# Attention and FFN layer on one core: V projected into token rows for two head pairs, output projection and next x's transposes as fillers, PV visits and fillers replanned

## What is computed

```python
q, k, v = x @ w_q, x @ w_k, x @ w_v                  # per head, 128 -> 64
probs   = softmax(q @ k.T / 8 + causal_mask)         # 1024 x 1024 per head
attn    = sum over heads of (probs @ v) @ w_o.T
x1      = layernorm(x + attn)
h       = butterfly(x1 @ W_exp + b_exp, up_weights)   # 9 stages over 512 features
y       = butterfly(gelu(h + up_bias), down_weights) @ W_con + b_con + down_bias
out     = layernorm(x1 + y)
```

## Time and profile before

| | |
|---|---|
| median of three runs | 1208.28 us |
| profiled execution | 1209.85 us, span of its instructions 1207.8 us |
| PE matmul busy | 1124.5 us, 93% of the span |
| PE weight loads busy | 725.1 us, 60% |
| DVE, ACT, POOL busy | 728.8, 650.3, 758.4 us (60%, 54%, 63%) |
| mean granted PE clock | 0.982 of full speed |
| chain that ended last | PE 69%, DMA 9%, issue 6%, DVE 6%, ACT 3%, POOL 3% |

### The profile page before, as it was taken

One profiled execution on the slowest core, in us unless ns is written; L12 is line 12 of the kernel. 1 busy time (PEld: TensorE's weight loads), 2 busy tenths in 40 slices (PEclk: granted clock), 3 DMA queues, 4 the chain that ended last, 5 costly groups with the idle time before them and its releaser, 6 DMA issues.

```text
span 1207.8 us, 18944 instructions
## 1 busy us (share of the span) xinstructions
PE 1124.5 (93%) x5880; PEld 725.1 (60%) x5880; DVE 728.8 (60%) x2029; ACT 650.3 (54%) x1294; POOL 758.4 (63%) x722
## 2 busy tenths in 40 slices
PE   5899999999899999999899999999899999998897
PEld 4566555665666656565765555665765556653666
DVE  5766666665666666664566666665466666650555
ACT  3466666663466666663366666664366566643231
POOL 6377777776377767676177777777176676667102
PEclk9899999999999999999999999999999999998999
DMA  6122222221222222221222221221122222110002
GB/s 197 36 68 67 54 71 71 54 72 37 61 54 66 69 54 71 72 53 36 61 63 54 71 71 48 68 62 38 45 63 71 53 48 51 47 36 18 10 9 61
DMA packets 63633, 69.83 MB, mean 58 GB/s; under 512 B 26759, under 2 KB 35243, under 8 KB 63534
## 3 DMA queue, kind: packets, MB, share of 16 engines
q1 hardware_dynamic: 63534, 68.64, 21.9%
HBM read 32.15 MB, written 2.36 MB: 29 GB/s over the span
## 4 chain that ended last, share of the span: by engine, by line
PE 69%; DMA 9%; issue 6%; DVE 6%; ACT 3%; SPq 3%; POOL 3%; DVEq 0%; POOLq 0%; ACTq 0%
PE O L683 14%; PE WORK L634 12%; PE SC L666 9%; PE SC L662 9%; PE WORK L722 5%; DMA QL<-NROW 4%; PE WORK L651 4%; PE WORK L614 3%; PE WORK L616 3%; PE WORK L622 3%; PE WORK L615 3%; PE WORK L778 3%; DMA R<-RROW 2%; DMA RROW<-RCOL 2%; SPq L394 2%
## 5 line engine op out<-in xcount | busy, mean ns | idle before, releaser
L867 ACT ACTIVATE PR<-SC 128x512 f32<-128x512 f32 (+3 forms) x768 | 351.4, 490 | 273.4 <-PE SC L666 254.5
L515 POOL TENSOR_TENSOR SUM<-SUM,PR 128x1024 f32<-128x1024 f32 (+3 forms) x256 | 416.9, 1628 | 10.1
L683 PE MATMUL O<-PR,VP 128*64 128x512 f32 (+3 forms) x1536 | 293.0, 500 | 3.7 <-POOL PR L500 3.7
L666 PE MATMUL SC<-QL,KH 128*128 128x512 f32 (+3 forms) x768 | 265.1, 351 | 19.6 <-DMA QL<-NROW 19.6
L662 PE MATMUL SC<-QH,KHL 128*128 128x512 f32 (+3 forms) x768 | 268.4, 355 | 5.4 <-ACT PR L867 4.3
L500 POOL TENSOR_SCALAR_AFFINE_SELECT PR<-PR 128x256 f32<-128x256 f32 x256 | 107.0, 418 | 262.4 <-ACT PR L867 261.9
L989 DVE CUSTOM_DVE_ANT_0 WORK<-WORK,CMASK 128x128 f32<-128x128 f32 (+3 forms) x512 | 240.2, 510 | 34.2 <-PE WORK L634 34.0
L634 PE MATMUL WORK<-KHL,QH 128*128 128x512 f32 (+3 forms) x768 | 233.5, 377 | 11.5 <-DVE MP L989 6.4
L992 DVE TENSOR_REDUCE MP<-WORK 128x1 f32<-128x512 f32 x256 | 165.0, 686 | 84.1 <-PE WORK L634 84.1
L634 PEld LDWEIGHTS WORK<-KHL,QH 128*128 128x128 f32 x768 | 136.2, 190 | 97.1 <-issue 54.4
L662 PEld LDWEIGHTS SC<-QH,KHL 128*128 128x128 f32 x768 | 145.5, 189 | 81.2 <-ACT PR L867 41.2
(11 more groups left out here) (95 smaller groups left out, 1052.7 us busy)
## 6 DMA issues: line engine op xcount, KB each, us to landing
QH<-QH SPq DMA_DIRECT2D x128, 128.0 KB, 2.3
KH<-KHL SPq DMA_DIRECT2D x128, 128.0 KB, 2.3
R<-RROW SPq DMA_DIRECT2D x128, 128.0 KB, 2.8
SW<-in_L_ffn_up_weights_dram SPq DMA_DIRECT2D x9, 512.0 KB, 4.6
SW<-_L_ffn_down_weights_dram SPq DMA_DIRECT2D x9, 512.0 KB, 4.8
RCOL<-R SPq DMA_DIRECT2D x128, 2.0 KB, 1.8
out_dram<-X SPq DMA_DIRECT2D x8, 256.0 KB, 2.3
QL<-NROW SPq DMA_DIRECT2D x64, 4.0 KB
```

Of the source, the lines that this page charges most:

```text
L515: nc.gpsimd.tensor_tensor(total, total, prob(unit, s), ALU.add).then_inc(add_done, 1)
L666: nc.tensor.matmul(dst, KH1[:, par, h, kt * P:(kt + 1) * P], QL[:, par, h, q0:q0 + n], start=False, stop=True).then_inc(scores_ready, 1)
L683: t = nc.tensor.matmul(O[qc][h * K:(h + 1) * K, START[s]:], VP[:, par, kt, h * K:(h + 1) * K], p[:, h, :], start=kt == 0, stop=s == LAST_O ...
L867: nc.scalar.activation(prob(unit, s)[:, h, :], SC[use % NSC][:, 0:n], ACT.Exp, scale=K ** -0.5).then_inc(exp_done, 1)
```

## The change

V is no longer projected for one pair into feature rows and transposed. A filler `v` uses x's high and low parts as the stationary operand and 256 columns of w_v (two pairs) as the moving one, so V comes out in token rows. Each unit makes half of the token tiles, for two pairs. `proj` 2 and `vt` go. The output projection of a sequence becomes four fillers `out` in the next sequence's first unit, the transposes of a later x become fillers `lay` in four units, and `flush` goes (the last sequence's work behind the last unit stays). `PV_AFTER`, `FILL`, `RECIP_AFTER` and `SCALE_AFTER` are new tables. The two DMAs of each half for `RCOL`, and the two for `R`, become one each. `compose` writes its products over the stage's weights, at steps 0, 6 and 7. The copy through `MVT` and the reload of x go.

```diff
-PV_AFTER = {1: [-3, -2, -1, 0], 3: [1], 6: [2, 3], 7: [4, 5], 9: [6, 7], 10: [8]}
+PV_AFTER = {1: [-3, -2, -1], 2: [0, 1], 6: [2, 3], 9: [4, 5, 6], 11: [7, 8]}
...
-FILL[1] = [[('proj', 2, 1), ('proj', 1, 1)], [], [('norm', 1, 1)] + MAXES[0:1]]
+FILL[1] = [[("proj", 1, 1)], [("v", 0)], [("norm", 1, 1)] + MAXES[0:1]]
...
-COMPOSE_AFTER = {1: 0, 3: 1}
-SCALE_AFTER = {5: (1, 1), 11: (0, 0)}
-RECIP_AFTER = {3: (1, 1), 8: (0, 0)}
+COMPOSE_AFTER = [0, 6, 7]
+SCALE_AFTER = {5: (1, 1), 10: (0, 0)}
+RECIP_AFTER = {2: (1, 1), 7: (0, 0)}
...
+OUT_AT = {0: (2, 2), 1: (4, 2), 2: (7, 2), 3: (9, 2)}
+LAY_AT = (8, 2)
...
+    if b > 0 and n == 0:
+        rows += [OUT_AT[i] + (("out", b - 1, i),) for i in OUT_AT]
+    if 0 < b < B - 1 and n < LAY_UNITS:
+        rows.append(LAY_AT + (("lay", b + 1, n),))
...
-                for h in range(2):
-                    sp.dma_start(R[h * K:(h + 1) * K, :], RROW[h:h + 1, :].broadcast_to([K, CH])).then_inc(inverse_landed, 16)
+                sp.dma_start(R[:, :], RROW.rearrange("(h a) n -> h a n", a=1).broadcast_to([2, K, CH])).then_inc(inverse_landed, 16)
...
-                elif f[0] == "vt":
-                    c = f[1]
-
-                    evacuated(numbers[("proj", 2 if c else 1, c)])
-                    for i in range(TPC):
-                        t = nc.tensor.transpose(w[:, i * P:(i + 1) * P], VT[:, c, i * P:(i + 1) * P], IDN[:])
+                elif f[0] == "v":
+                    unit, _, tile = v_units(u)
+                    if f[1] == 0:
+                        pe.wait_ge(v_weights_lo, unit // 2 + 1)
+                    for i in range(2):
+                        lo = tokens_of(unit) + (tile + 2 * f[1] + i) * P
+                        out = w[:, i * 2 * P:(i + 1) * 2 * P]
+                        nc.tensor.matmul(out, XTH[:, lo:lo + P], WSV[:, 0, :], start=True, stop=False)
+                        nc.tensor.matmul(out, XTH[:, lo:lo + P], WSV[:, 1, :], start=False, stop=False)
+                        t = nc.tensor.matmul(out, XTL[:, lo:lo + P], WSV[:, 0, :], start=False, stop=True)
...
+                elif f[0] == "lay":
+                    for i in range(2):
+                        t = nc.tensor.transpose(w[:, i * P:(i + 1) * P], X[:, f[1] * TILES + 2 * f[2] + i, :], IDN[:])
+                elif f[0] == "out":
+                    _, b, i = f
+
+                    pe.wait_ge(o_free, ((b + 1) * PAIRS - 1) * CHUNKS + i * OUT_TILES // TPC + 1 + O_CREDIT)
+                    for k in range(OUT_TILES):
+                        tok = (i * OUT_TILES + k) * P
+                        for pr in range(PAIRS):
+                            t = nc.tensor.matmul(w[:, k * P:(k + 1) * P], OT[:, pr, tok:tok + P], WOT[:, pr, :],
+                                                 start=pr == 0, stop=pr == PAIRS - 1)
...
+                elif f[0] == "v":
+                    unit, slots, tile = v_units(u)
+                    if f[1] == 0 and u > 0:
+
+                        act.wait_ge(pv_done, (u - u % 2) * NS + PV_CREDIT)
+                    V = VHI if tile else VLO
```

More of the change, by code:

```diff
@@ L112 @@
+LAST_PROJ = ("proj", 1, 1)
 assert sum(f[0] == "max" for _, _, f in FILLERS) == len(MAXES)
-NWORK = 4
[L114 to L121, removed]
-NSC = 2
-assert 2 * NS % NSC == 0
@@ L126 @@
[L126 to L148, removed]
+STAGE_UNIT = [1 + 5 * n // 3 for n in range(2 * STAGES + 1)]
@@ new lines @@
+COMPOSE = {}
+for n in range(2 * STAGES):
+    for part in range(3):
+        unit = STAGE_UNIT[n] + (part == 2 and STAGE_UNIT[n + 1] > STAGE_UNIT[n] + 1)
+        COMPOSE.setdefault((unit, COMPOSE_AFTER[0 if unit > STAGE_UNIT[n] else part]), []).append(3 * n + part)
+assert all(len(ops) == 1 for ops in COMPOSE.values()) and max(unit for unit, _ in COMPOSE) < UNITS
+NWORK = 4
+LAY_UNITS = TILES // 2
+OUT_AT = {0: (2, 2), 1: (4, 2), 2: (7, 2), 3: (9, 2)}
+LAY_AT = (8, 2)
+OUT_TILES = TILES // len(OUT_AT)
@@ L152, in butterfly_op, with fillers_at @@
+LAST_NORM = n
+LAST_OUT = n + 1
+def fillers_at(u, s, place):
+    return [(f, n) for at, p, f, n in SCHEDULE[u] if (at, p) == (s, place)]
+NSC = 2
+assert 2 * NS % NSC == 0 and LAST_PROJ in PREFETCH
+def butterfly_op(eng, y, sides, w, stage, rows, part):
     s, width = 2 ** stage, y.shape[-1]
@@ L284, in post_norm_layer, with tokens_of, v_units, values @@
         out_tiles = out.rearrange("b (t p) d -> p (b t) d", p=P)
[L287 to L333, removed]
+        def tokens_of(u):
+            return u // PAIRS % 2 * S
+        def v_units(u):
+            return (u + 1, 4, 0) if u % 2 else (u, 2, TPC)
+        def values(u, kt):
+            return VLO[:, u % 4, kt, :] if kt < TPC else VHI[:, u % 2, kt - TPC, :]
         def keys_of(part, qt):
@@ L647, in norm @@
                 _, qc, before = f
[L649 removed]
+                pe.wait_ge(add_done, ((unit - before) * NA + (adds_until(LAST_OF[qc] + 1) + ADD_CREDIT)))
                 for h in range(2):
@@ L668, in scores, with fill, pv @@
                     if h == 0:
-                        between()
-            def pv(unit, par, s):
+                        fill(unit, s, BETWEEN)
+            def fill(u, s, place):
+                for f, n in fillers_at(u, s, place):
+                    filler(u, f, n)
+            def pv(unit, s):
                 qc, kt = STEPS[s]
@@ L691, in window @@
                 for s in range(NS):
-                    def fill(place):
-                        for f, n, ahead in [(f, n, ahead) for at, p, f, n, ahead in queue if (at, p) == (s, place)]:
-                            filler(f, base + n, unit + (ahead - 1), (par + ahead) % 2, tokens_of(b, j, par, ahead), numbers)
-                    scores(unit, par, s, lambda: fill(BETWEEN))
-                    fill(BEHIND)
+                    scores(u, s)
+                    fill(u, s, BEHIND)
                     for ps in PV_AFTER.get(s, []):
@@ L751, in _ @@
             pe.wait_ge(laid_copied, len(LAY) + 1)
-            sweep(pe, window, flush)
+            for u in range(UNITS):
+                window(u)
+            for s in PV_LEFT:
+                pv(UNITS - 1, s)
+            norm(("norm", 1, 0), take_work(LAST_NORM), UNITS - 1)
+            for i in OUT_AT:
+                filler(UNITS, ("out", B - 1, i), LAST_OUT + i)
             def transpose_x1(g):
@@ L1106, in _ @@
-            sweep(dve, window, flush)
+            for u in range(UNITS):
+                window(u)
+            recip(UNITS - 1, 1)
+            for i in OUT_AT:
+                if i == 2:
+                    scale(UNITS - 1, 1)
+                    dve.wait_ge(rstd_made, 1)
+                    for g in range(AHEAD):
+                        normalise(g, x1_made)
+                consume(UNITS, ("out", B - 1, i), LAST_OUT + i)
             def residual(g):
```

493 lines of the change are left out of this document (227 added, 266 removed).

## The result

| | before | after |
|---|---|---|
| median | 1208.34 us (4 runs, 1206.38 to 1210.69) | 1236.21 us (4 runs, 1233.07 to 1238.49) |
| profiled span | 1207.8 us | 1235.0 us |
| PE busy | 1124.5 us, 93% | 1101.9 us, 89% |
| mean granted PE clock | 0.982 | 0.964 |

The changed kernel is slower: ratio 1.0228, 95% interval 1.0198 to 1.0258. The forecast was 1125 us, range 1114 to 1150. PE's records shrank by 22.6 us, yet the span grew by 27.2: PE now stands still for 133.1 us instead of 83.3.

A forecast was written before the change was run, and what follows sets the result against it. PE, busy 93% of the span, was taken as the bound. Gains of 23.9 + 10.5 + 21 + 7 + 24 less 2.9 made 83.5 us, giving 1125 us; own range 1115 to 1136, with four rivals 1114 to 1150.

The forecast's parts named there:

- The merged DMAs: On SP's queue, the joined DMAs for `RCOL` and `R` save one issue per hop, priced at 0.
- V: In V's projection on PE, eight transposes per unit go; net 0.77 us in 31 units, 23.9 us won.
- The rival that weight loads pace them: Weight loads pace V's new 256-column matmuls, so 23.9 us are not won: 1149 us, chance 0.06.
- `QL`: Copying `NROW` ahead of Q's low part ends PE's wait before the second scores matmul: 21 us, bounds 0 and 27.
- DVE's banks: Earlier reciprocal and scaling free `WORK` banks for the maxima on PE: 7 us won, bounds 10 won to 10 lost.
- A group fewer: One PV group fewer per unit on PE saves a float32 mode change, 0.34 us in 31 units: 10.5 us.
- Flushes: At sequence boundaries, three flushes go: 24 us won; the fillers' own mode changes lose 2.9 us.
- the wait only moves: Rival: another chain closes in the faster unit, at DVE's earlier reciprocal or `QL`: 1147 to 1160 us, chance 0.08.
- POOL: Rival: POOL's masks come late and PE's first PV waits; possibly slower than before, 1249 us at 7 us late; chance 0.04.

The follow-up runs named there:

- Experiment 7: Four transposes of a constant tile put ahead of each `v`, against the changed kernel with the `R` broadcast issued per head: 1127.44 us.
- experiment 12: `QL`'s small DMAs issued ahead of each unit's second `R` broadcast, against the changed kernel with `R` still merged: 1294.66 us.
- experiment 9: PV visits set back to the places of the kernel before, against the changed kernel with the `R` broadcast issued per head: 1141.80 us.
- experiment 2: Only the broadcast into `R` issued per head again, `RCOL`'s DMA still merged, against the changed kernel: 1100.62 us.
- experiment 11: PV visits, reciprocals, second scaling and Q's low part all set back as before, against the changed kernel with `R` per head: 1215.82 us.

## Why the prediction was wrong, step by step

- **The step that failed** is the sentence "The merged DMAs take one issue out of each hop and I price them at 0." Two edits stood under it. `RCOL`'s is a gain of 5.7 us with `R` split; `R`'s costs 135.6 us in this kernel and 338 us in the one before. No row of before showed such a broadcast with two outermost; it should have had bounds from both sides. The nearest row was the old form's, 2.8 us for 128 KB, and I did not ask what the new form does to the number of engines. What the runs show in the place of the 0: `R` releases DVE 7.3 us behind its issue instead of 3.4, `QL` behind it in 5.1 instead of 2.6, and PE stands 133.1 us instead of 40.2. Without this edit the change gives 1100.62 us, 24 us better than the forecast and also outside its range, so the other terms were too small in sum.
- **V**: right. The twelve matmuls stand 0.12 us apart after the change, and the transposes are worth 26.8 us with a change of mode (0.86 per unit, forecast 0.83 and 0.1). The rival that weight loads pace them is refuted by these starts, as the loads of these matmuls are recorded with some 192 ns each. With it falls what the prediction drew from the Trainium skill ("Perfetto Trace Analysis", "Identifying the Most-Contended Engine"), that the busy share of LDWEIGHTS tells how close TensorE is to its limit. Experiment 7 alone would not tell, as its transposes bring loads of their own.

```profile
632.75 0.28 PE L590 MATMUL WORK<-WSV,XTH 128*128 128x256 f32 x1
632.87 0.28 PE L591 MATMUL WORK<-WSV,XTH 128*128 128x256 f32 x1
632.99 0.28 PE L592 MATMUL WORK<-WSV,XTL 128*128 128x256 f32 x1
633.11 0.29 PE L590 MATMUL WORK<-WSV,XTH 128*128 128x256 f32 x1
```

- **`QL`**: the mechanism was right, and undone by `R`. With `R` split the copy stands 0.31 us behind `mt` (615.30 and 615.61, forecast 0.35), and PE has 3.97 us of work until the waiting matmul (619.27, forecast 3.9). All of the wait goes, not 21 of 26.9. With `R` merged, the sentence "SP reaches this DMA only after the second half's `R`" held the danger: not because SP comes late, but because `QL` then lands only with `R` (experiment 12).
- **DVE's banks**: with `R` split the maxima's wait is gone, so the whole 6.4 us and their restarts are won. DVE does block at the reciprocal, as feared, for 1.4 us in 27 of 30 waits (60.2 us in all, 23 of them in the three last), and PE does not feel it.
- **A group fewer**: the price of 0.34 us stands; that the visits also cover ACT was missed (experiment 9).
- **Flushes**: the forecast had 24 won and 2.9 lost, 21 net. In experiment 2 the units start at

```profile
238.29 2.73 PE O L671 x12
...
266.89 2.73 PE O L671 x12
...
307.04 2.73 PE O L671 x12
...
339.39 2.73 PE O L671 x12
```

  that is 28.6 us for a unit and 72.5 for the two that hold the projection of a sequence: 15.3 us above two plain units, 15.3 and 14.9 at the other two boundaries. Before, the second boundary had 87.3 - 62.8 = 24.5, but the first and the third, by the same rows, only 21.1 and 21.2 (265.94 to 349.83 and 813.77 to 897.75). That is 66.8 against 45.5, 21.3 won; the four units with a `lay` outside these pairs take 28.8 and give 0.7 back. With the 0.9 for each boundary that the prediction adds, since no `QL` wait stood behind a flush, it is about 23 net: the term was right. Its sum of the losses is 3.1, not 2.9 (2.04 + 3.68 - 1.6 - 1.02), which changes nothing.
- **The sum**: a unit takes 28.6 us, not 29.4. Forecast, and what the rows give, by part: V 24 and about 25, group 10.5 and 10.5, `QL` 21 and 27, banks 7 and about 11 (6.4, and a restart estimated at 0.3 for each of 16), flushes 21 and 23. These sum to 96.5 of the 107.7 us between 1208.34 and 1100.62; the other 11 I have not assigned, and they are nearly half of the 24 us by which the forecast was too cautious. Only V's part has an experiment of its own (7); the others are read from rows, not measured apart.
- **The rivals**: "the wait only moves" (8%) is nearest to what happened, since `QL`'s wait stayed and the maxima's grew, but its cause was not in it, and its 1147 to 1160 are far off. POOL was no cause: PE waits 4.1 us for its masks in 3 waits after, 3.7 in 5 before.

## What to carry to other kernels

A DMA that is rewritten for fewer issues is a new transfer: look at its outermost dimension before pricing it. Here 2 in the source, in one DMA, cost 136 us against 64 in two, and 4 cost 19. An edit whose form no row of the profile shows gets bounds, not a zero, above all where its landing stands one or two microseconds ahead of a waiting engine: up to that slack it costs little, beyond it each microsecond is paid in every unit and once more in PE's clock. A price found by taking one part out of a tuned plan belongs to that plan alone.

## What the runs showed of the hardware that was not expected

- One broadcast of 256 KB from HBM with two outermost keeps 0.13 of the DMA engines busy, moves 51 GB/s and takes 6.8 to 8.3 us from issue to the reader's start (median 7.3); the same bytes as two DMAs with four outermost give 0.25, 96 GB/s and 5.3 us, with 64 outermost 0.49, 184 GB/s and 3.4 us (shares and rates in a 1 us window).
- Two DMAs of 128 KB with two outermost each take longer than the one of 256 KB (median 8.75 against 7.3 us), with slices at 25 GB/s.
- A DMA of 4 KB issued 2.9 us behind such a broadcast lands with it: PE starts 0.36 to 0.46 us behind the start of the scaling in 19 of the 24 waits of the changed kernel, and has no wait at all once it is issued first. The Trainium skill's statement ("DMA: Bandwidth & Descriptors", "Why a DMA increments its semaphore by 16 and not by 1"), that a DMA issued by SP takes the lowest-numbered engines, fits that; no row here shows engine numbers.
- The lower clock does not always begin at the stop's end. In experiment 11 the matmuls behind a stop of 2.26 us follow each other by 0.43 us at once, at a granted clock of 0.50, the 1.2 GHz level. In the changed kernel, behind one of 2.40 us, they keep 0.23 for 0.9 us, and then take 0.42 for some 3 us (granted clock 0.50 from 409 to 412), before they are back at 0.99. So a stop also costs behind its end: the profile's idle time is only a part of it.

```profile
407.63 0.38 PE L604 MATMUL WORK<-KHL,QH 128*128 128x256 f32 x1 [2.40 <-DVE MP L953]
407.86 0.40 PE L645 MATMUL SC<-QH,KHL 128*128 128x512 f32 x1
...
408.95 0.63 PE L649 MATMUL SC<-QL,KH 128*128 128x512 f32 x1
409.37 1.27 PE L604 MATMUL WORK<-KHL,QH 128*128 128x512 f32 x3
```
